# The value product moved behind both score and maximum pairs of a slot, gates of half the tokens, and a projection in four pieces

## The chip, the cores and the metric

One NeuronCore of one Trainium2 chip runs the whole program. The metric is the device time of one launch in microseconds, lower is better. TensorE (PE), VectorE (DVE), ScalarE (ACT) and GpSimd (POOL) each run their own instructions strictly as written, and wait for each other on semaphores; SyncE (SP) issues the transfers.

## The reference

Four sequences of 512 tokens with 128 features pass two layers. In each layer the normalized input goes to an attention and to a feed-forward part, and both are added to the input:

```python
xn = _layernorm(x)
x = x + attn_0(xn) + ffn_0(xn)      # 16 heads of 8, bias; gated feed-forward, hidden 384
xn = _layernorm(x)
x = x + attn_1(xn) + moe(xn)        # 16 heads of 8, block mask; 8 experts of 256, top 2
```

Attention is `softmax(q k^T / sqrt(8)) v` and a projection. The first feed-forward part is `(silu(x Wg) * (x Wu)) Wd`. The second sends each token to the two experts of eight that its router prefers. All is in float32.

## The kernel before

**Units and slots.** The work is cut into eight units (`U = 2 * B`): unit `u` is the attention of sequence `u % 4` in layer `u // 4`. Each unit has 16 slots (`SLOTS_U`), and a slot handles two groups of two heads for one block of 128 keys. In a slot TensorE makes two score pairs (`score_mms`, line 747, two matmuls each, S0 and S1 below), ScalarE takes the exponential of each pair (`exponential`, line 962), and TensorE multiplies the exponentials of the slot before with the values (`value_mms`, line 763, called V below). The exponential needs the maximum of each row beforehand, so in the same slots TensorE makes the scores of a later part a first time (`max_mms`, line 732, M0 and M1 below) and VectorE reduces each pair (`read_max`, line 1114). Maxima run ahead: 24 pairs before the first slot, then two in each slot up to slot 3 of unit 7.

**Three pairs of PSUM banks in turn.** Scores, maxima, gates and expert products all write to banks 0 to 5, in pairs that are handed out in the order of a list, `taken`. Before a job takes a pair, TensorE waits until the job three places earlier in the list has been read:

```python
taken.append(("score", 2 * (SLOTS_U * u + slot) + jj))
if len(pairs_at(u, slot)) > jj:
    taken.append(("max", pairs_at(u, slot)[jj]))
```

So the list reads S0 M0 S1 M1 and then a gate or two expert jobs, if the slot has any. V writes to a bank of its own (6), and all small work (transposes, q, k and v, the projection, routing) goes through bank 7, `SIDE`, at the end of a slot.

**The order on TensorE** is written out by hand in `tensor_unit`: S0, M0, V of the slot before, S1, M1, the gate, expert jobs, and last `side_mms`. In slot 6 two tiles of the projection of the unit before (`out_mms`, lines 822 and 825) stand between V and S1, and the two other tiles at the end of the slot.

**Gates.** In layer 0 each unit has three gate jobs (`gate_up_0`, lines 785 and 786, `HB = 3` blocks of the hidden layer, 512 tokens wide) in slots 9, 10 and 11. ScalarE makes half a tanh (`half_tanh`, line 978), VectorE the rest (`gated`, lines 1135 and 1150), in the slot's last place on both engines.

**ScalarE and VectorE** follow the slots: on ScalarE the first exponential, a copy from bank 7 if there is one, the second exponential, later copies and the tanh; on VectorE the maximum of M0, small work, the maximum of M1, the gate. In slot 6 ScalarE's copy is that of the row maxima (`maxima_copy`, line 955), and the first tile of the projection waits for it, since it overwrites bank 7.

**SyncE's queue** issues all loads of weights before unit 0's own transfers; the last three of `loads` are the experts' weights (`eg`, `eu`, `ed`, 1 MB each), and `max_rows` of unit 0 comes behind them.

**Experts.** From slot 4 of unit 6 each slot has two expert jobs (`expert_work_at`), to slot 11 of unit 7: transposes of gathered tokens (`places_mms`), gates of 320 places (`gate_up_1`, lines 802 and 803) and the output product (`expert_out`, line 810), which ScalarE copies in five pieces (`result_copy`, line 994). In unit 7 from slot 4 there are no maxima.

Of the kernel before, what the change touches and what calls it, by code (L numbers as in the profile page):

```python
# [12 lines left out]
P = 128  # L13
# [4 lines left out]
def build(nc, x, wq, wk, wv, bq, bk, bv, wo, bo, wg_T, wu_T, wd_T, src_blocks, tgt_blocks, router_T, eg_T, eu_T,  # L18
# [4 lines left out]
    U = 2 * B  # L23
# [28 lines left out]
    with ExitStack() as ctx:  # L52
# [114 lines left out]
        emptied = sem("emptied")  # L167
        empty_ready = sem("empty_ready")
        loaded = sem("loaded")
        x_loaded = [sem(f"x_loaded{b}") for b in range(B)]  # L170
        zeros = sem("zeros")
        consts = sem("consts")
# [106 lines left out]
        def pairs_at(u, slot):  # L279

            q = LEAD + PAIRS_U * u + 2 * slot
            return [v for v in (q, q + 1) if v < N_PAIRS]

        def gate_at(u, slot):

            return HB * u + slot - 9 if u < B and 9 <= slot < 9 + HB else None


        expert_work = [("places", 0), ("places", 1)] + [("gate1", m) for m in range(4)]
# [157 lines left out]
        def sync_unit(sp, u):  # L447
            p, n = u + 2, u + 1
            if u == U - 2:
                for e in range(2):  # L450
                    load_places(sp, e)
                load_meta(sp)
                for e in range(2, 4):
                    load_places(sp, e)
            max_rows(sp, u, 1)
            if p < U:
                operand_writes(sp, p, 0)
                operand_writes(sp, p, 1)
                if layer(p) == 0:
                    operand_reads_0(sp, p)  # L460
                else:
                    operand_reads_1(sp, p, 0)
            if u == U - 2:
                for e in range(4, 7):
                    load_places(sp, e)
            if n < U:
                max_rows(sp, n, 0)
            if u == U - 2:
                load_places(sp, 7)
            if p < U and layer(p) == 1:  # L470
                operand_reads_1(sp, p, 1)
            if u < 2:
                empty_places(sp, u)
# [304 lines left out]
            last.then_inc(onT_ps, 1)  # L778

        def gate_up_0(pe, g):  # L780
            u, i = g // HB, g % HB
            pe.wait_ge(ready, 1)
            pair = take_pair(pe, "gate0", g)
            cols = slice(i * P, (i + 1) * P)
            pe.matmul(ps[:, 2 * pair, :], wg[:, cols], xnT[u % 4][:], start=True, stop=True).then_inc(gate_ps[0], 1)  # L785
            pe.matmul(ps[:, 2 * pair + 1, :], wu[:, cols], xnT[u % 4][:], start=True, stop=True).then_inc(up_ps[0], 1)  # L786

        def places_mms(pe, e):
            pe.wait_ge(places_in[e % 2], 16 * (e // 2 + 1))
# [5 lines left out]
        def gate_up_1(pe, g):  # L795

            e, i, c = g // 4, g % 4 // 2, g % 2
            pe.wait_ge(loaded, N_LOAD)
            pe.wait_ge(places_ready, e + 1)
            pair = take_pair(pe, "gate1", g)  # L800
            cols, x_T = slice(i * P, (i + 1) * P), places_T[e % 2][:, c * HALF:(c + 1) * HALF]
            pe.matmul(ps[:, 2 * pair, 0:HALF], eg[:, e, cols], x_T, start=True, stop=True).then_inc(gate_ps[1], 1)  # L802
            pe.matmul(ps[:, 2 * pair + 1, 0:HALF], eu[:, e, cols], x_T, start=True, stop=True).then_inc(up_ps[1], 1)  # L803
# [10 lines left out]
        def out_mms(pe, u, tiles):  # L814
            L = layer(u)
            if tiles[0] == 0:
                pe.wait_ge(onT_ready, u + 1)
                if L == 0:
                    pe.wait_ge(h_ready[0], HB * (u + 1))
            for t in tiles:  # L820
                tok = slice(t * P, (t + 1) * P)
                last = pe.matmul(ps[:, SIDE, tok], o_T[:, tok], w_proj[L][:], start=True, stop=(L == 1))  # L822
                if L == 0:
                    for i in range(HB):
                        last = pe.matmul(ps[:, SIDE, tok], h0_T[:, i, tok], wd[:, i, :], start=False,  # L825
                                         stop=(i == HB - 1))
            if tiles[-1] == NT - 1:
                last.then_inc(y_ps, 1)
# [14 lines left out]
        def side_mms(pe, u, slot):  # L843
# [23 lines left out]
                    pe.wait_ge(qk_f_ready, 2 * p + 2)  # L867
                max_transposes(pe, u, 1)
            if slot == 6 and u >= 1:
                out_mms(pe, w, (2, 3))  # L870
            if slot == 7 and p < U and layer(p) == 1:
                pe.wait_ge(unit_done, u)
                rank_mms(pe, p)
            if slot == 8 and n < U:
                pe.wait_ge(mT_ready, 2 * u + 2)
                pe.wait_ge(unit_done, u)
                if p < U and layer(p) == 1:
                    pe.wait_ge(rank_read, seq(p) + 1)
                v_mms(pe, n, SIDE)
            if slot == 10:  # L880
                pe.wait_ge(unit_done, u)
                if n < U:
                    pe.wait_ge(v_read, n + 1)
                out_transposes(pe, u, 0)
            if slot == 11 and f < U:
                pe.wait_ge(on_ready, 2 * u + 1)
# [12 lines left out]
        def tensor_unit(pe, u):  # L899
# [3 lines left out]
            for slot in range(SLOTS_U):  # L903
# [3 lines left out]
                score_mms(pe, u, slot, 0)  # L907
                if maxima:
                    max_mms(pe, maxima[0])
                if u > 0 or slot > 0:  # L910
                    value_mms(pe, SLOTS_U * u + slot - 1)
                if slot == 6 and u >= 1:
                    pe.wait_ge(mT_ready, 2 * u + 2)
                    out_mms(pe, u - 1, (0, 1))
                score_mms(pe, u, slot, 1)
                if maxima:
                    max_mms(pe, maxima[1])
                if gate_at(u, slot) is not None:
                    gate_up_0(pe, gate_at(u, slot))
                for kind, n in expert_work_at(u, slot):  # L920
# [48 lines left out]

        def half_tanh(act, L, g):  # L970

            n = S if L == 0 else HALF
            act.wait_ge(gate_ps[L], g + 1)
            if g >= 2:
                act.wait_ge(h_ready[L], g - 1)
            elif L == 1:
                act.wait_ge(h_ready[0], HB * B)
            act.activation(th[:, g % 2, 0:n], ps[:, 2 * pair_of(f"gate{L}", g), 0:n], ACT.Tanh, scale=0.5).then_inc(  # L978
                tanh_done[L], 1)

# [38 lines left out]
        def scalar_unit(act, u):  # L1019
            w, n, p, f = u - 1, u + 1, u + 2, u + 3  # L1020
            for slot in range(SLOTS_U):
# [13 lines left out]
                    xnT_copy(act, f, SIDE)  # L1035
                if slot == 14 and n < U:
                    maxima_copy(act, n, 0)
                if slot == 8 and p < U and layer(p) == 1:
# [90 lines left out]
            last.then_inc(on_ready, 1)  # L1129

        def gated(dve, L, g):
            n, bank = S if L == 0 else HALF, 2 * pair_of(f"gate{L}", g)
# [4 lines left out]
            dve.wait_ge(gate_done[L], g + 1)  # L1137
            dve.wait_ge(up_ps[L], g + 1)
            if L == 0:
                if g % HB == 0 and g > 0:  # L1140
                    dve.wait_ge(y_ps, g // HB)
                dst = h0_T[:, g % HB, :]
            else:
                e = g // 4
                if g == 0:
# [38 lines left out]
        def vector_unit(dve, u):  # L1184
            w, n, f = u - 1, u + 1, u + 3
            for slot in range(SLOTS_U):
# [2 lines left out]
                    read_max(dve, maxima[0])  # L1189
                if slot == 2 and u >= 1:  # L1190
                    normalize_out(dve, w, 1)
                if slot == 7 and u >= 1:
                    residual(dve, w)
                if slot == 8 and f < U:
                    statistics(dve, f)
                if slot == 9 and n < U:
                    read_v(dve, n, SIDE)
# [3 lines left out]
                    read_logits(dve, f)  # L1201
                if maxima:
                    read_max(dve, maxima[1])
                if gate_at(u, slot) is not None:
                    gated(dve, 0, gate_at(u, slot))
                for kind, m in expert_work_at(u, slot):
# [3 lines left out]
        def last_vector(dve):  # L1210
            normalize_out(dve, U - 1, 1)
            for b in range(B):
# [16 lines left out]
                 (w_router[:], router_T), (eg[:], eg_T), (eu[:], eu_T),  # L1229
                 (ed[:], ed_T.rearrange("e (b p) d -> p e b d", p=P))]  # L1230
        N_LOAD, N_FIRST = 16 * len(loads), 16 * len(first_loads)
# [279 lines left out]
```

## Time and profile before

| what | value |
|---|---|
| median of three runs | 543.98 us (542.29 to 545.46) |
| the profiled execution's own time | 544.03 us |
| its span, first to last instruction | 542.0 us |
| TensorE busy | 454.8 us (84%) |
| VectorE busy | 400.5 us (74%) |
| ScalarE busy | 328.8 us (61%) |
| GpSimd busy | 262.5 us (48%) |
| granted TensorE clock, mean | 0.95 |

The first score pair starts at 50.0 us, slot 4 of unit 7 at 472.3 us. Busy time counts a matmul to its modelled end, while the next one can start before that. A slot is found in the timeline by its order S0, M0, V, S1, M1.

### The profile page before, as it was taken

Reading aid. Unit: us, or ns where it says so; the run is one execution under the profiler, and the core shown is the slowest. Engines: PE = TensorE matmul, PEld = TensorE weight load, DVE = VectorE, ACT = ScalarE, POOL = GpSimd, SP = SyncE. Lnnn points to the kernel's source line nnn. Section 1 sums busy time; section 2 is a strip of 40 time slices with the busy share of each in tenths; the row PEclk is TensorE's granted clock in tenths of the full one; section 3 lists DMA queues with packets and bytes.
Section 4 is the critical chain, followed back from the end, with each engine's and each line's share of the span. In section 5 each row is a group of like instructions: output and inputs, shape, how many; then the busy total and the mean of one; then the engine's idle time right before and its main releaser. Section 6 shows DMA issues by size and latency. Waiting matters only on the chain.

```text
span 542.0 us, 9302 instructions
## 1 busy us (share of the span) xinstructions
PE 454.8 (84%) x3394; PEld 169.4 (31%) x3394; DVE 400.5 (74%) x538; ACT 328.8 (61%) x422; POOL 262.5 (48%) x499
## 2 busy tenths in 40 slices
PE   3456979889988999899989898987899999999952
PEld 1101213224322433242312431221245453455511
DVE  5699778886998699869887798789876777623204
ACT  2102666776677667656676577777766567667560
POOL 6861263724425562886378657884201233163240
PEclk9755889999999999999999999999999999999995
DMA  3896596244511360626252645174731111010018
GB/s 82 238 230 89 89 343 106 93 163 146 90 43 61 118 62 4 66 72 127 25 52 39 157 43 56 41 160 68 109 52 32 45 50 50 4 44 25 21 47 219
DMA packets 143742, 48.27 MB, mean 89 GB/s; under 512 B 109890, under 2 KB 139090, under 8 KB 142866
## 3 DMA queue, kind: packets, MB, share of 16 engines
q1 hardware_dynamic: 141394, 42.93, 38.1%
q0 software_dynamic: 2304, 4.76, 2.6%
q8 instruction: 27, 0.44, 0.3%
q14 instruction: 17, 0.14, 0.1%
HBM read 22.81 MB, written 23.14 MB: 85 GB/s over the span
## 4 chain that ended last, share of the span: by engine, by line
PE 53%; DVE 18%; issue 10%; ACT 10%; DMA 4%; SPq 4%; POOL 1%; POOLq 0%; ACTq 0%; DVEq 0%
PE ps L763 14%; DVE mx L1114 11%; PE ps L747 9%; PE ps L732 7%; ACT PT L962 6%; PE ps L802 3%; PE ps L810 3%; PE ps L785 2%; PE ps L803 2%; SPq L433 2%; PE ps L693 2%; PE ps L825 2%; PE ps L822 2%; PE ps L786 1%; DVE th L1135 1%
## 5 line engine op out<-in xcount | busy, mean ns | idle before, releaser
L1114 DVE TENSOR_REDUCE mx<-ps 128x2 f32<-128x1024 f32 x256 | 309.4, 1223 | 73.1 <-PE ps L732 65.1
L962 ACT ACTIVATE PT<-ps 128x1024 f32<-128x1024 f32 x256 | 258.6, 1026 | 125.9 <-PE ps L747 116.5
L763 PE MATMUL ps<-PT,Vp 128*32 128x512 f32 x1024 | 138.1, 611 | 5.4 <-ACT PT L962 4.4
L732 PE MATMUL ps<-KO,QO 48*128 48x512 bf16 (+1 forms) x512 | 104.5, 406 | 39.7 <-ACT PT L962 22.6
L747 PE MATMUL ps<-QO,KO 59*128 59x512 bf16 x512 | 100.2, 390 | 3.8 <-DMA QO<-mT 2.5
L520 POOL DMA_INDIRECT y_tokens<-expert_io,meta x40 | 38.6, 964 | 71.5 <-ACT expert_io L994 48.5
L747 PEld LDWEIGHTS ps<-QO,KO 59*128 59x128 bf16 x512 | 24.6, 93 | 142.8 <-issue 87.9
L1135 DVE SCALAR_TENSOR_TENSOR th<-th,ps 128x320 f32<-128x320 f32 (+1 forms) x44 | 23.8, 541 | 35.2 <-ACT th L978 29.4
L732 PEld LDWEIGHTS ps<-KO,QO 48*128 48x128 bf16 (+1 forms) x512 | 25.6, 96 | 70.9 <-ACT PT L962 38.6
L545 POOL CAST mp<-mx 128x32 bf16<-128x32 f32 x16 | 3.4, 214 | 82.9 <-DVE mx L1114 78.7
L509 POOL DMA_INDIRECT x_places<-xe,place_i x32 | 31.9, 995 | 22.3 <-ACT PT L962 15.2
L763 PEld LDWEIGHTS ps<-PT,Vp 128*32 128x32 f32 x1024 | 20.4, 108 | 45.7 <-issue 39.7
L978 ACT ACTIVATE th<-ps 128x320 f32<-128x320 f32 (+1 forms) x44 | 21.1, 487 | 12.0 <-PE ps L802 5.8
L802 PE MATMUL ps<-expert_io,eg 128*128 128x320 f32 x64 | 24.4, 462 | 2.1 <-ACT expert_io L994 0.6
L1150 DVE SCALAR_TENSOR_TENSOR h_all<-th,ps 128x320 f32<-128x320 f32 (+1 forms) x44 | 23.8, 541 | 1.5
L955 ACT COPY mT<-ps 24x512 bf16<-24x512 bf16 x16 | 9.0, 562 | 26.1 <-PE ps L739 26.1
L492 POOL TENSOR_SCALAR xe<-xs,mv,rstd 128x128 f32<-128x128 f32 x28 | 22.2, 802 | 0.8
L994 ACT ACTIVATE expert_io<-ps,meta 128x128 f32<-128x128 f32 x40 | 11.2, 372 | 18.6 <-PE ps L810 18.6
L803 PE MATMUL ps<-expert_io,eu 128*128 128x320 f32 x64 | 22.4, 432 | 0.0
L810 PE MATMUL ps<-ed,h_all 128*128 128x128 f32 x160 | 19.4, 276 | 1.2 <-DVE h_all L1150 1.2
L810 PEld LDWEIGHTS ps<-ed,h_all 128*128 128x128 f32 x160 | 18.9, 192 | 3.0 <-DVE h_all L1150 1.7
L1120 DVE RECIPROCAL rden<-ps 128x32 f32<-128x32 f32 x16 | 5.6, 349 | 16.3 <-PE ps L771 16.3
(166 smaller groups left out, 475.1 us busy)
## 6 DMA issues: line engine op xcount, KB each, us to landing
z<-part SPq DMA_DIRECT2D x16, 384.0 KB
z<-part SPq DMA_DIRECT2D x16, 256.0 KB
QO<-z SPq DMA_DIRECT2D x64, 48.0 KB
KO<-z SPq DMA_DIRECT2D x64, 48.0 KB
x_places<-expert_io SPq DMA_DIRECT2D x2, 1300.0 KB, 7.4
expert_io<-x_places SPq DMA_DIRECT2D x8, 320.0 KB, 3.5
QO<-z SPq DMA_DIRECT2D x6, 384.0 KB
KO<-z SPq DMA_DIRECT2D x6, 384.0 KB
```

The lines of the kernel that those rows point to most:

```text
L509: pool.indirect_dma_start(out=x_places[:], out_offset=bass.IndirectOffsetOnAxis(ap=place_i[:, b, t, k:k + 1], axis=0), in_=xe[p % 2][:, t, ...
L520: pool.indirect_dma_start(out=y_tokens[:], out_offset=bass.IndirectOffsetOnAxis(ap=meta[:].bitcast(I32)[:, e, j, 0:1], axis=0), in_=y_sb[e ...
L732: mm = pe.matmul(ps[:, 2 * pair + half, :], rows_of(QO[u % 3], half, 2 * s + jj, rows, (qt, qt + 1)), rows_of(KO[u % 3], half, 2 * s + jj, ...
L747: mm = pe.matmul(ps[:, 2 * pair + half, :], rows_of(KO[u % 3], half, 2 * s + jj, ROWS, (k, k + 1)), rows_of(QO[u % 3], half, 2 * s + jj, R ...
L763: last = pe.matmul(ps[32 * g:32 * g + 32, PV_BANK, :], Vp[u % 2][:, k, head(s, g), :], PT[:, (2 * t + g % 2) % 4, g // 2, :], start=(s % 2 ...
L802: pe.matmul(ps[:, 2 * pair, 0:HALF], eg[:, e, cols], x_T, start=True, stop=True).then_inc(gate_ps[1], 1)
L803: pe.matmul(ps[:, 2 * pair + 1, 0:HALF], eu[:, e, cols], x_T, start=True, stop=True).then_inc(up_ps[1], 1)
L810: last = pe.matmul(across(pair, j * P, (j + 1) * P), h1_T[:, e % 2, i, j * P:(j + 1) * P], ed[:, e, i, :], start=(i == 0), stop=(i == EB - 1))
L962: act.activation(PT[:, e % 4], ps[:, 2 * pair:2 * pair + 2, :], ACT.Exp).then_inc(exp_done, 1)
L1114: dve.tensor_reduce(mx[:, a, qt, col:col + 5:4], ps[:, 2 * pair:2 * pair + 2, :], AX_X, ALU.max, negate=True).then_inc(max_read, 1)
L1135: dve.scalar_tensor_tensor(out=t, in0=t, scalar=1.0, in1=ps[:, bank, 0:n], op0=ALU.add, op1=ALU.mult).then_inc(gate_done[L], 1)
L1150: dve.scalar_tensor_tensor(out=dst, in0=t, scalar=0.5, in1=ps[:, bank + 1, 0:n], op0=ALU.mult, op1=ALU.mult).then_inc(h_ready[L], 1)
```

## The change

On TensorE, V moves from between M0 and S1 to behind M1, in all slots. The list `taken` keeps its order for scores and maxima.

Each gate job of layer 0 becomes two, for 256 tokens each, and the six stand in slots 10 to 15 in place of three in slots 9 to 11.

For the projection of a layer 0 unit (`spread(u)`, units 1 to 4) the four tiles go to four places: tile 0 in slot 6 between M0 and S1, tile 1 at the end of slot 6, tiles 2 and 3 at the same places of slot 7. With it the residual sum moves from slot 7 to 8, the statistics behind the second maximum of slot 8, and the routing's rank matmuls from slot 7 to 9 (their copy from slot 8 to 10), with the waits that bank 7 then needs. For a layer 1 unit two tiles stand between M0 and S1 of slot 6 and two at its end, as before.

The experts' weights get a semaphore of their own and are loaded in units 0 (`eg`, `eu`) and 1 (`ed`), behind `operand_writes`.

```diff
+        G0, N_TOK0, GATE_SLOT = 2 * HB, S // 2, SLOTS_U - 2 * HB
+        def spread(u):
+            return u >= 1 and layer(u - 1) == 0
+        def rank_slot(u):
+            return 9 if spread(u) else 7
         def gate_at(u, slot):
-            return HB * u + slot - 9 if u < B and 9 <= slot < 9 + HB else None
+            return G0 * u + slot - GATE_SLOT if u < B and slot >= GATE_SLOT else None
...
                 operand_writes(sp, p, 1)
+                if u < 2:
+                    for dst, src in expert_loads[0:2] if u == 0 else expert_loads[2:3]:
+                        sp.dma_start(dst, src).then_inc(experts_loaded, 16)
...
         def gate_up_0(pe, g):
-            u, i = g // HB, g % HB
+            u, i, c = g // G0, g % G0 // 2, g % 2
...
-            pe.matmul(ps[:, 2 * pair, :], wg[:, cols], xnT[u % 4][:], start=True, stop=True).then_inc(gate_ps[0], 1)
+            cols, x_T = slice(i * P, (i + 1) * P), xnT[u % 4][:, c * N_TOK0:(c + 1) * N_TOK0]
+            pe.matmul(ps[:, 2 * pair, 0:N_TOK0], wg[:, cols], x_T, start=True, stop=True).then_inc(gate_ps[0], 1)
...
             if slot == 6 and u >= 1:
-                out_mms(pe, w, (2, 3))
-            if slot == 7 and p < U and layer(p) == 1:
+                out_mms(pe, w, (1,) if spread(u) else (2, 3))
+            if slot == 7 and spread(u):
+                out_mms(pe, w, (3,))
+            if slot == rank_slot(u) and p < U and layer(p) == 1:
                 pe.wait_ge(unit_done, u)
+                if slot > 8:
+                    pe.wait_ge(v_read, n + 1)
                 rank_mms(pe, p)
...
                 if maxima:
                     max_mms(pe, maxima[0])
-                if u > 0 or slot > 0:
-                    value_mms(pe, SLOTS_U * u + slot - 1)
                 if slot == 6 and u >= 1:
                     pe.wait_ge(mT_ready, 2 * u + 2)
-                    out_mms(pe, u - 1, (0, 1))
+                    out_mms(pe, u - 1, (0,) if spread(u) else (0, 1))
+                if slot == 7 and spread(u):
+                    out_mms(pe, u - 1, (2,))
                 score_mms(pe, u, slot, 1)
                 if maxima:
                     max_mms(pe, maxima[1])
+                if u > 0 or slot > 0:
+                    value_mms(pe, SLOTS_U * u + slot - 1)
                 if gate_at(u, slot) is not None:
...
-                if slot == 7 and u >= 1:
+                if slot == (8 if spread(u) else 7) and u >= 1:
                     residual(dve, w)
-                if slot == 8 and f < U:
+                if slot == 8 and f < U and not spread(u):
                     statistics(dve, f)
...
                 if maxima:
                     read_max(dve, maxima[1])
+                if slot == 8 and f < U and spread(u):
+                    statistics(dve, f)
```

## Rows read from the trace of the kernel before

**Rows 1.** The page, part 1: busy time of each engine and share of the span.
```profile
PE 454.8 (84%) x3394; PEld 169.4 (31%) x3394; DVE 400.5 (74%) x538; ACT 328.8 (61%) x422; POOL 262.5 (48%) x499
```

**Rows 2.** Windows: stretch, its length, each engine's busy us, TensorE's clock, DMA share, GB/s.
```profile
49.96:105.90 55.94, 48.68 (x292) 12.59 (x292) 46.11 (x52) 36.27 (x42) 25.01 (x56) 0.90 0.57 139
105.90:161.70 55.80, 51.22 (x346) 17.49 (x344) 46.50 (x57) 38.06 (x45) 19.75 (x41) 1.00 0.42 119
105.90:378.00 272.10, 245.17 (x2032) 81.76 (x2030) 224.57 (x281) 186.71 (x217) 161.07 (x328) 1.00 0.42 83
378.00:472.30 94.30, 88.28 (x685) 41.31 (x683) 72.22 (x100) 62.85 (x95) 20.69 (x31) 1.00 0.27 51
472.30:513.50 41.20, 38.24 (x243) 22.11 (x241) 12.54 (x28) 26.32 (x46) 17.33 (x18) 1.00 0.09 30
513.50:525.50 12.00, 7.64 (x58) 1.40 (x56) 0.00 (x0) 9.04 (x13) 6.73 (x7) 1.00 0.11 38
```

**Rows 3.** Waits of TensorE's matmuls, 50 to 472.3 us: total us, times, longest.
```profile
PE ps L732 <- ACT PT L962: 22.6, 40, 0.8
...
PE ps L747 <- DMA QO<-mT: 2.5, 1, 2.5
...
PE ps L732 <- DMA QO<-mask_q: 0.2, 1, 0.2
```

**Rows 4.** Timeline, unit 1's end: start, duration, engine, instructions merged, idle before.
```profile
161.20 0.39 PE L747 MATMUL ps<-QO,KO 59*128 59x512 bf16 x2
161.43 0.38 PE L732 MATMUL ps<-KO,QO 48*128 48x512 bf16 x2
161.63 1.94 ACT L962 ACTIVATE PT<-ps 128x1024 f32<-128x1024 f32 x2 [0.77 <-PE ps L747]
161.74 0.39 PE L747 MATMUL ps<-QO,KO 59*128 59x512 bf16 x2
161.85 2.52 DVE L1114 TENSOR_REDUCE mx<-ps 128x2 f32<-128x1024 f32 x2 [0.31 <-PE ps L732]
...
162.71 0.39 PE L732 MATMUL ps<-KO,QO 48*128 48x512 bf16 x2 [0.58 <-ACT PT L962]
163.03 1.06 PE L763 MATMUL ps<-PT,Vp 128*32 128x512 f32 x8
...
164.03 0.39 PE L747 MATMUL ps<-QO,KO 59*128 59x512 bf16 x2
```

**Rows 5.** Timeline, the slot behind an expert output product, 431 to 435 us.
```profile
431.58 0.39 PE L747 MATMUL ps<-QO,KO 59*128 59x512 bf16 x2
431.69 1.40 ACT L994 ACTIVATE expert_io<-ps,meta 128x128 f32<-128x128 f32 x5 [2.33 <-PE ps L810]
...
432.95 1.96 ACT L962 ACTIVATE PT<-ps 128x1024 f32<-128x1024 f32 x2
...
434.06 0.39 PE L732 MATMUL ps<-KO,QO 56*128 56x512 bf16 x2 [0.52 <-ACT PT L962]
434.38 0.81 PE L802 MATMUL ps<-expert_io,eg 128*128 128x320 f32 x2
```

**Rows 6.** Timeline, slot 6 of unit 6, 399 to 402 us.
```profile
399.01 0.39 PE L747 MATMUL ps<-QO,KO 59*128 59x512 bf16 x2
...
400.37 0.56 ACT L955 COPY mT<-ps 24x512 bf16<-24x512 bf16 x1
...
400.98 0.71 PE L822 MATMUL ps<-w_proj,o_T 128*128 128x128 f32 x4 [0.36 <-ACT mT L955]
```

**Rows 7.** Windows on the clock: the stretch behind the DMA wait, and the end of unit 1.
```profile
78.00:84.00 6.00, 6.00 (x38) 1.85 (x36) 4.87 (x12) 3.37 (x4) 3.24 (x5) 0.73 0.97 251
157.80:165.50 7.70, 5.79 (x46) 1.16 (x38) 6.64 (x6) 5.92 (x9) 4.91 (x9) 1.00 0.47 179
```

**Rows 8.** Lines with shapes kept apart: gate matmul and VectorE's first gate step.
```profile
L785 PE MATMUL ps<-xnT,wg 128*128 128x512 f32 x24 | 13.2, 632 | 2.2 <-DVE mx L1114 2.2
...
L1135 DVE SCALAR_TENSOR_TENSOR th<-th,ps 128x512 f32<-128x512 f32 x12 | 8.3, 688 | 3.6 <-ACT th L978 3.3
```

More of the change, by code:

```diff
@@ L169, in build @@
         loaded = sem("loaded")
+        experts_loaded = sem("experts_loaded")
         x_loaded = [sem(f"x_loaded{b}") for b in range(B)]
@@ L780, in gate_up_0 @@
         def gate_up_0(pe, g):
-            u, i = g // HB, g % HB
+            u, i, c = g // G0, g % G0 // 2, g % 2
             pe.wait_ge(ready, 1)
             pair = take_pair(pe, "gate0", g)
-            cols = slice(i * P, (i + 1) * P)
-            pe.matmul(ps[:, 2 * pair, :], wg[:, cols], xnT[u % 4][:], start=True, stop=True).then_inc(gate_ps[0], 1)
-            pe.matmul(ps[:, 2 * pair + 1, :], wu[:, cols], xnT[u % 4][:], start=True, stop=True).then_inc(up_ps[0], 1)
+            cols, x_T = slice(i * P, (i + 1) * P), xnT[u % 4][:, c * N_TOK0:(c + 1) * N_TOK0]
+            pe.matmul(ps[:, 2 * pair, 0:N_TOK0], wg[:, cols], x_T, start=True, stop=True).then_inc(gate_ps[0], 1)
+            pe.matmul(ps[:, 2 * pair + 1, 0:N_TOK0], wu[:, cols], x_T, start=True, stop=True).then_inc(up_ps[0], 1)
         def places_mms(pe, e):
@@ L797, in gate_up_1 @@
             e, i, c = g // 4, g % 4 // 2, g % 2
-            pe.wait_ge(loaded, N_LOAD)
+            pe.wait_ge(experts_loaded, N_EXPERT)
             pe.wait_ge(places_ready, e + 1)
@@ L818, in out_mms @@
                 if L == 0:
-                    pe.wait_ge(h_ready[0], HB * (u + 1))
+                    pe.wait_ge(h_ready[0], G0 * (u + 1))
             for t in tiles:
@@ L876, in side_mms @@
                 pe.wait_ge(unit_done, u)
-                if p < U and layer(p) == 1:
+                if p < U and layer(p) == 1 and rank_slot(u) < slot:
                     pe.wait_ge(rank_read, seq(p) + 1)
@@ L883, in side_mms @@
                     pe.wait_ge(v_read, n + 1)
+                if p < U and layer(p) == 1:
+                    pe.wait_ge(rank_read, seq(p) + 1)
                 out_transposes(pe, u, 0)
@@ L970, in half_tanh @@
         def half_tanh(act, L, g):
-            n = S if L == 0 else HALF
+            n = N_TOK0 if L == 0 else HALF
             act.wait_ge(gate_ps[L], g + 1)
@@ L976, in half_tanh @@
             elif L == 1:
-                act.wait_ge(h_ready[0], HB * B)
+                act.wait_ge(h_ready[0], G0 * B)
             act.activation(th[:, g % 2, 0:n], ps[:, 2 * pair_of(f"gate{L}", g), 0:n], ACT.Tanh, scale=0.5).then_inc(
@@ L1037, in scalar_unit @@
                     maxima_copy(act, n, 0)
-                if slot == 8 and p < U and layer(p) == 1:
+                if slot == rank_slot(u) + 1 and p < U and layer(p) == 1:
                     ranks_copy(act, p)
@@ L1131, in gated @@
         def gated(dve, L, g):
-            n, bank = S if L == 0 else HALF, 2 * pair_of(f"gate{L}", g)
+            n, bank = N_TOK0 if L == 0 else HALF, 2 * pair_of(f"gate{L}", g)
             t = th[:, g % 2, 0:n]
@@ L1139, in gated @@
             if L == 0:
-                if g % HB == 0 and g > 0:
-                    dve.wait_ge(y_ps, g // HB)
-                dst = h0_T[:, g % HB, :]
+                if g % G0 == 0 and g > 0:
+                    dve.wait_ge(y_ps, g // G0)
+                dst = h0_T[:, g % G0 // 2, g % 2 * N_TOK0:(g % 2 + 1) * N_TOK0]
             else:
@@ L1228, in build @@
                  (w_proj[1][:], wo[1]), (b_proj[1][:], bo[1][None, :].to_broadcast([P, D])),
-                 (w_router[:], router_T), (eg[:], eg_T), (eu[:], eu_T),
-                 (ed[:], ed_T.rearrange("e (b p) d -> p e b d", p=P))]
-        N_LOAD, N_FIRST = 16 * len(loads), 16 * len(first_loads)
+                 (w_router[:], router_T)]
+        expert_loads = [(eg[:], eg_T), (eu[:], eu_T), (ed[:], ed_T.rearrange("e (b p) d -> p e b d", p=P))]
+        N_LOAD, N_EXPERT, N_FIRST = 16 * len(loads), 16 * len(expert_loads), 16 * len(first_loads)
         def load_x(sp, b):
```

## The prediction

> **What bounds the kernel now.** I read the page first: TensorE is busy 84% of the span, VectorE 74%, ScalarE 61% [rows 1]. No engine is full, so the order of the waits decides. The windows by stretch come next: in unit 1 TensorE is busy 51.22 of 55.80 us and VectorE 46.50 [rows 2], so both are near the end of what they have, and 4.58 us are TensorE's idle time. The waits of TensorE say what that idle time is. Between 50 and 472.3 us the view has 18 rows with 84 waits and 39.9 us in sum, first among them M0's wait for an exponential (40 times, 22.6 us) [rows 3].
>
> The timeline shows the loop behind that wait [rows 4]. S1 is issued at 161.20, ScalarE starts on it at 161.63, TensorE issues M1 at 161.43 and the next S0 at 161.74, then waits until 162.71 for M0, because M0 takes the pair that S1 held. The reader should take four lengths from these rows. A score pair needs 0.23 us until the next pair can be issued (161.20 to 161.43). From a score pair's issue to the issue of the pair that waits for its exponential it is 1.51 us (161.20 to 162.71). From a pair that waited to V it is 0.32 us, and V lasts 1.00 us until the next issue (163.03 to 164.03). The loop S1, exponential, M0, V, S1 is 1.51 + 0.32 + 1.00 = 2.83 us, and TensorE is idle in it unless side work fills the time.
>
> **The change part by part: V behind M1.** By the list `taken`, M0 takes the pair of the S1 before it, and M1 takes the pair of S0 of its own slot (three places back in S0 M0 S1 M1). So M1 can't be issued sooner than 1.51 us behind S0. Before, S0, M0, V and S1 stand ahead of it: 0.23 + 0.32 + 1.00 + 0.23 = 1.78 us, and that wait costs nothing. V is its cover. The trace shows the wait bare in one kind of slot, behind an expert output product: the exponential of S0 starts only after five copies, and M1 is idle 0.52 us for it although V stood ahead of it [rows 5].
>
> After, only S0, M0 and S1 stand ahead of M1, 0.69 us, so TensorE idles some 0.8 us in every slot that has maxima. V is queued behind M1 and can't fill this, nor can the gate, the expert jobs or the side work; and S0 of the next slot is behind all of them. The new loop is S0, exponential, M1, V, gate and side work, next S0: 2.83 us plus all the rest that the slot issues. The old loop is gone, since M0 now comes later than S1's exponential, but it only bound where side work was short; the new one has side work in series.
>
> Without idle time a slot's own five jobs take 0.23 + 0.32 + 1.00 + 0.23 + 0.23 = 2.01 us now, and 2.83 us after: 0.82 us more. There are 116 slots with maxima (units 0 to 6, four of unit 7); the first has no V, which leaves 115 x 0.82 = 94.3 us. From this goes TensorE's present idle time in the same slots: (55.94 - 48.68) + (272.10 - 245.17) + (94.30 - 88.28) = 40.2 us [rows 2]. The idle times are counted from the modelled end of a matmul, 0.39 us, while the next could be issued after 0.23 [rows 4], so each of the 84 waits hides 0.16 us more: 13.4 us. Net: 94.3 - 40.2 - 13.4 = **+40.7 us**. For unit 1 alone, with its ten waits (1.6 us), this gives 51.22 - 1.6 + 16 x 0.82 = 62.7 against 55.80 us.
>
> I take 0.32 us from the pair that waited to V, as the row has it. The Trainium skill (TensorE: Matmul & The Clock Gate, Part 2, step by step) says that TensorE's queue pulls weight loads ahead of matmuls in flight while matmuls keep their order; if V's first weights came early in that way the step would be 0.23, and 115 x 0.09 = 10 us less would give 580. The row speaks against it here.
>
> **Small terms.** (a) In the slot behind an expert output product among those with maxima (four: products in slots 8, 11, 14 of unit 6 and 1 of unit 7) S0 to the first expert job takes 2.80 us now [rows 5]; with V behind M1 it is 3.80, not 2.83: 4 x 0.97 = +3.9. (b) Slot 6: the first projection tiles wait for the row maxima's copy, 1.97 us from S0 [rows 6]; V covered that. In units 5 and 6 the two tiles take 0.71 us, and M1 is issued at 1.97 + 0.71 + 0.23 = 2.91 where the sum has 1.51 + 0.71: +0.7 each, +1.4. In units 1 to 4 a tile has four products, where two products take 0.71 us in the row, so at most 1.4 us; I take 1. Slot 6 loses 0.7 there too, and tile 2 in slot 7 fills the new gap and gives 0.7 back: 0. The split helps only by that. (c) The output copy of slot 0 now starts behind the later V, 0.32 + 1.00 us after M1. A ScalarE copy takes 0.56 us [rows 6], so it ends at 1.88 and with the step to ScalarE at about 1.97, when S0's exponential could start at 1.32 + 0.39 = 1.71: 0.26 us late, seven times: +1.8. (d) In units 1 to 4 the residual and the statistics stand together in VectorE's slot 8 and reach slot 10's maximum late: estimated at 0.4 each, +1.5, with bounds of nothing and one maximum's read, 1.26 [rows 4]. (e) The end, slots 12 to 15 of unit 7, has no maxima; there V ahead of S1 stands in the loop to S1's exponential, and four slots take 12.00 us with 9.04 of ScalarE [rows 2]. After, ScalarE alone bounds, and at most 3.0 us are to be had; the last V has to wait in both orders, so I take less than half, -1.3. (f) The experts' loads no longer stand ahead of `max_rows` of unit 0: the 2.5 us wait goes [rows 3] (it is in the 40.2 already), and with it the time at the lower clock behind it, 0.73 granted in 78 to 84 us [rows 7], (1 - 0.73) x 6.0 = 1.6: -1.6. What waits behind the loads in their new place are unit 2's operand reads and unit 1's row maxima; unit 2's maxima begin at slot 4 of unit 1, past 105.9 us, and the loads are issued in the middle of unit 0. Without that distance the cost would be of the size of the 2.5 us wait.
>
> **Gates in halves.** The matmul columns stay. A half can't take less than half nor more than the whole of 632 ns and 688 ns [rows 8]; I take the lower end plus a little, 0.42 us for each of VectorE's two steps: 12 x 0.42 - 6 x 0.69 = +0.9 us of VectorE per unit, hidden: VectorE has 46.5 busy us in a unit that will last over 60. On TensorE 0 to +3 us over four units; I take 0. The rank matmuls wait for the values' read in slot 9, three units, under 0.3 each: inside (d). Slots 4 to 11 of unit 7 issue the same work in another order and nearly fill TensorE (38.24 of 41.20 [rows 2]): 0, bounds -2 and +2.
>
> Sum: 40.7 + 3.9 + 1.4 + 1.8 + 1.5 - 1.3 - 1.6 = +46.4. The profiled execution took 544.03 us (542.0 of span and 2 around it), which is the median of the runs (543.98). 544.0 + 46.4 = 590.4, and I say **590 us**.
>
> **The rivals.** *Faster: the pair of S0 is free when M1's turn comes.* It decides where 1.51 us or more lie between S0 and M1 without a wait. Then the slot costs 2.01 us and its side work, M0's 22.6 us of waits go [rows 3], VectorE's 0.31 us before each pair too [rows 4], and with the 2.5 and 1.6 of the loads and the 1.3 of the end the time is 544.0 - 28.0 = 516. For it: VectorE idles at present, and S1 and M1 come earlier. Against it: ScalarE's 0.97 us an exponential [rows 4] lies in S0's own slot, and only slots 6 and 7 put anything there. I give it 5 in 100; with 3 more for gains and losses that cancel.
>
> *Smaller: the expert slots escape.* If their gates and copies already pace them so that M1's gap replaces other waits, 20 slots x 0.82 and (a) drop out: 590 - 20 = 570. Against it: TensorE is idle only 6.02 of 94.30 us there [rows 2]. 12 in 100.
>
> *Larger: the clock falls.* TensorE's new gaps of 0.8 us would have it granted 1.2 GHz in part of the time. It had 48.68 + 245.17 + 88.28 = 382 busy us in the slots with maxima [rows 2]; were a tenth of that work at the lower clock, it would take 38 us more: 628. Against it: between 157.8 and 165.5 us TensorE is busy 5.79 of 7.70 us, with a gap in each slot, at clock 1.00 [rows 7]. 8 in 100. The Trainium skill (the same page, A second HAM failure mode: psum-queue depth-cycling) tells of a kernel that cycles through PSUM banks and whose small gaps between groups of matmuls made the clock swing; by that rule this change, with more gaps, is a case for it. The trace so far disagrees, at 1.00 in gaps of that size.
>
> *The move of the loads does nothing*, if another transfer holds the maxima's rows: +4 us, inside the range.
>
> **How the numbers follow.** The forecast has 72 in 100, with its own range of 576 to 606: lower if the step from M1 to V is 0.23 us, as between two other pairs (10 us), and by the bounds of small terms, higher by gates (+3), waits that add up in slots with long side work, and an uneven VectorE. The other cases are 12 (570), 8 (628), 5 (516) and 3 (no change). To leave no more than 2 in 10 outside, the range reaches down to the smaller case: 568 to 606. A measurement of this kernel can tell about 0.5% from no change, 2.7 us. Faster 5, same 3, slower 92 in 100.
>
> **What would show it.** In the profile after: M1 idle before it for ScalarE in nearly every slot with maxima, some 0.6 us in the view's count, over 100 times; M0 waiting for ScalarE no more; slots 0, 3, 5 of a unit over 2.83 us; unit 1 near 62 us; TensorE's busy time nearly unchanged and its share near 77%; slot 6's first tile idle about 1.4 us for the row maxima's copy; no wait for row maxima's transfer in unit 0. The prediction is wrong if M1 is issued right behind S1, or if the clock of the middle stretches is below 1.00.

## Result and the profile after

The change makes the kernel slower: 585.46 us (584.7 to 586.17, four runs) against 544.16 us in the same comparison, a ratio of 1.076 with a 95% interval of 1.073 to 1.080. The forecast was 590, with a range of 568 to 606. The profiled execution has a span of 583.6 us, 41.6 more than before.

The page of the changed kernel, parts 1 and 4: busy time, and the chain that ended last by engine.

```profile
PE 460.2 (79%) x3442; PEld 183.2 (31%) x3442; DVE 403.6 (69%) x562; ACT 327.3 (56%) x434; POOL 261.5 (45%) x499
...
PE 59%; ACT 20%; DVE 9%; issue 7%; DMA 2%; POOL 1%; SPq 1%; POOLq 0%; ACTq 0%; DVEq 0%
```

TensorE's busy time is up by 5 us only [rows 1]; its share fell from 84% to 79%, so what was added is waiting. On the chain ScalarE has 20%, before 10%. Windows of the changed kernel by the same stretches as in [rows 2] (length, busy us of TensorE, weight loads, VectorE, ScalarE, GpSimd, clock, DMA):

```profile
49.96:108.53 58.57, 48.95 (x306) 15.17 (x306) 46.99 (x58) 37.37 (x45) 28.06 (x67) 0.94 0.54 134
108.53:171.17 62.64, 52.53 (x358) 20.17 (x356) 47.34 (x64) 38.08 (x47) 19.51 (x34) 1.00 0.42 124
108.53:408.10 299.57, 246.85 (x2066) 90.77 (x2064) 227.77 (x301) 185.63 (x225) 157.60 (x316) 1.00 0.39 75
408.10:512.00 103.90, 89.01 (x685) 42.13 (x683) 71.19 (x100) 61.66 (x94) 20.59 (x31) 1.00 0.24 46
512.00:555.40 43.40, 39.28 (x243) 22.44 (x241) 12.38 (x27) 26.42 (x47) 17.02 (x18) 0.96 0.08 29
```

| stretch | before | after | difference | the forecast's terms |
|---|---|---|---|---|
| unit 0 | 55.94 | 58.57 | +2.6 | +1.7 |
| units 1 to 5 | 272.10 | 299.57 | +27.5 | +33.1 |
| unit 6 and unit 7 to slot 3 | 94.30 | 103.90 | +9.6 | +12.9 |
| unit 7, slots 4 to 11 | 41.20 | 43.40 | +2.2 | 0 |
| the rest | 78.5 | 78.2 | -0.3 | -1.3 |

(The last column deals the terms of the sum out to their stretches, +46.4 in all. The bounds in the rows lie 0.17 us behind the first score pairs of their stretches; the lengths are right.) The loss is in every stretch that has maxima, and 2.2 us of it in slots of unit 7 that have none. The waits of TensorE's matmuls in the changed kernel, 50 to 512 us, answer to [rows 3]:

```profile
PE ps L746 <- ACT PT L984: 51.8, 83, 0.9
PE ps L836 <- ACT mT L977: 8.1, 6, 1.4
PE ps L761 <- DVE h_all L1172: 7.0, 16, 0.5
```

The first row looks like the old one, 51.8 us in place of 22.6, but it is another wait. In the timeline (slot 1 of unit 2, against [rows 4]) it is seen which:

```profile
173.82 0.39 PE L761 MATMUL ps<-QO,KO 59*128 59x512 bf16 x2
173.96 0.59 ACT L990 COPY o_sb<-ps 128x512 f32<-128x512 f32 x1 [0.49 <-PE ps L777]
174.05 0.38 PE L746 MATMUL ps<-KO,QO 48*128 48x512 bf16 x2
174.28 0.39 PE L761 MATMUL ps<-QO,KO 59*128 59x512 bf16 x2
174.44 1.95 ACT L984 ACTIVATE PT<-ps 128x1024 f32<-128x1024 f32 x2
...
175.52 0.39 PE L746 MATMUL ps<-KO,QO 48*128 48x512 bf16 x2 [0.85 <-ACT PT L984]
175.84 1.07 PE L777 MATMUL ps<-PT,Vp 128*32 128x512 f32 x8
...
176.84 0.66 PE L785 MATMUL ps<-ident,o_sb 128*128 128x128 f32 x4
177.43 0.39 PE L761 MATMUL ps<-QO,KO 59*128 59x512 bf16 x2
```

S0, M0 and S1 are issued 0.23 us apart, then TensorE idles until S0's exponential has ended, issues M1 at 175.52, V, the side work (0.59 us) and only then the next S0. M0 waits no more. Here the gap is 0.85 us, since the output copy, behind the later V, held up S0's exponential; in slots without it the gap reads 0.68. The slots with no side work are 2.83 us long: slot 0 of units 1 to 6, slots 14 and 15 of units 4 and 5, and a few more. Most others have that plus their side work; slot 6 and the expert slots have other waits too.

### The profile page after: what moved, and what is told of

Same layout as the page of the kernel before. It is cut to its first block, busy times and chain, and to the rows that moved or that the text cites. A ratio compares the mean times of both kernels' runs of the same rounds, so it can differ in the third digit from the quotient of the medians.

```text
span 583.6 us, 9474 instructions
## 1 busy us (share of the span) xinstructions
PE 460.2 (79%) x3442; PEld 183.2 (31%) x3442; DVE 403.6 (69%) x562; ACT 327.3 (56%) x434; POOL 261.5 (45%) x499
## 4 chain that ended last, share of the span: by engine, by line
PE 59%; ACT 20%; DVE 9%; issue 7%; DMA 2%; POOL 1%; SPq 1%; POOLq 0%; ACTq 0%; DVEq 0%
PE ps L777 20%; ACT PT L984 17%; PE ps L746 7%; PE ps L761 7%; DVE mx L1136 5%; PE ps L824 3%; PE ps L816 3%; PE ps L799 3%; PE ps L707 2%; PE ps L817 2%; PE ps L839 2%; PE ps L836 2%; PE ps L800 2%; DMA h_all<-y_tokens 1%; PE ps L785 1%
## 5 line engine op out<-in xcount | busy, mean ns | idle before, releaser
L984 ACT ACTIVATE PT<-ps 128x1024 f32<-128x1024 f32 x256 | 255.8, 1027 | 125.6 <-PE ps L761 117.3
L746 PE MATMUL ps<-KO,QO 48*128 48x512 bf16 (+1 forms) x512 | 104.5, 406 | 69.0 <-ACT PT L984 51.8
L761 PE MATMUL ps<-QO,KO 59*128 59x512 bf16 x512 | 98.6, 387 | 16.0 <-DVE h_all L1172 7.0
L1157 DVE SCALAR_TENSOR_TENSOR th<-th,ps 128x320 f32<-128x320 f32 (+1 forms) x56 | 25.7, 459 | 58.7 <-ACT th L1000 50.3
L1000 ACT ACTIVATE th<-ps 128x320 f32<-128x320 f32 (+1 forms) x56 | 23.1, 418 | 39.6 <-PE ps L799 23.5
L1172 DVE SCALAR_TENSOR_TENSOR h_all<-th,ps 128x320 f32<-128x320 f32 (+1 forms) x56 | 25.7, 459 | 1.9
L836 PE MATMUL ps<-w_proj,o_T 128*128 128x128 f32 x64 | 13.9, 327 | 10.9 <-ACT mT L977 9.7
```

The costliest lines, as they stand in the source:

```text
L746: mm = pe.matmul(ps[:, 2 * pair + half, :], rows_of(QO[u % 3], half, 2 * s + jj, rows, (qt, qt + 1)), rows_of(KO[u % 3], half, 2 * s + jj, ...
L761: mm = pe.matmul(ps[:, 2 * pair + half, :], rows_of(KO[u % 3], half, 2 * s + jj, ROWS, (k, k + 1)), rows_of(QO[u % 3], half, 2 * s + jj, R ...
L984: act.activation(PT[:, e % 4], ps[:, 2 * pair:2 * pair + 2, :], ACT.Exp).then_inc(exp_done, 1)
L1172: dve.scalar_tensor_tensor(out=dst, in0=t, scalar=0.5, in1=ps[:, bank + 1, 0:n], op0=ALU.mult, op1=ALU.mult).then_inc(h_ready[L], 1)
```

## Experiments

All of them change only the order, the place or the size of pieces, or repeat one; times stand beside runs of the kernel before on the same chip.

| run | median us | ratio to before, 95% |
|---|---|---|
| V behind M1 alone | 585.93 | 1.078 (1.074 to 1.082) |
| all but V | 536.58 | 0.987 (0.984 to 0.991) |
| changed kernel, V between S1 and M1 | 567.5 | 1.044 (1.040 to 1.048) |
| kernel before, V between S1 and M1 | 568.75 | 1.045 (1.040 to 1.050) |
| loads alone | 540.69 | 0.994 (0.992 to 0.996) |
| gates alone | 539.81 | 0.992 (0.990 to 0.995) |
| projection alone | 547.27 | 1.006 (1.004 to 1.008) |
| kernel before, V between S0 and M0 | 592.92 | 1.090 (1.086 to 1.095) |
| changed kernel, S1 three times | 598.26 | 1.100 (1.097 to 1.103) |
| changed kernel, V early in slot 6 | 578.2 | 1.063 (1.059 to 1.066) |
| V by the kind of slot | 536.95 | 0.988 (0.985 to 0.990) |
| loads and gates | 533.51 (before: 538.94 there) | 0.990 (0.988 to 0.992) |

**V behind M1 alone.**

```diff
                 if maxima:
                     max_mms(pe, maxima[0])
-                if u > 0 or slot > 0:
-                    value_mms(pe, SLOTS_U * u + slot - 1)
...
                 if maxima:
                     max_mms(pe, maxima[1])
+                if u > 0 or slot > 0:
+                    value_mms(pe, SLOTS_U * u + slot - 1)
```

> The kernel before with one edit: V is issued behind M1 in every slot. Theory (M1 waits for the exponential of its own slot's S0, and V was what stood in that time): the same loop of 2.83 us plus side work in every slot with maxima, so unit 1 at 61 to 63 us as in the changed kernel, and 585 to 597 us in all, since the loads' wait in unit 0 (2.5 us) and both first projection tiles between M0 and S1 of slot 6 stay. Rival (the gates in halves and the moved routing and loads carry a part of the loss): 544 to 570 us, unit 1 under 59 us.

585.93 us: the whole loss, with the gates, the projection and the loads untouched. Unit 1 lasts 62.50 us, within 0.2 of the changed kernel. A slot without side work in its timeline, TensorE only:

```profile
170.43 0.39 PE L747 MATMUL ps<-QO,KO 59*128 59x512 bf16 x2
170.66 0.38 PE L732 MATMUL ps<-KO,QO 48*128 48x512 bf16 x2
170.88 0.38 PE L747 MATMUL ps<-QO,KO 59*128 59x512 bf16 x2
171.94 0.39 PE L732 MATMUL ps<-KO,QO 48*128 48x512 bf16 x2 [0.68 <-ACT PT L962]
172.26 1.07 PE L763 MATMUL ps<-PT,Vp 128*32 128x512 f32 x8
173.26 0.39 PE L747 MATMUL ps<-QO,KO 59*128 59x512 bf16 x2
```

From S0 to M1 it is 1.51 us, to V 0.32, to the next S0 1.00: the 2.83 us of the forecast, term for term.

**All but V.** The diff is the change's own without the two hunks above.

> The changed kernel with V back between M0 and S1, everything else of the change kept. Theory: the loss is gone, 536 to 546 us: 4 us from the loads' wait and the lower clock behind it, and the halved gates and the split projection worth between 4 us of gain and 2 of loss. M1's wait for ScalarE is gone and M0's is back. Rival (the other parts carry a part of the loss): 555 to 585 us.

536.58 us, faster than the kernel before by 1.3%. The loss comes with V's move alone. And what the other parts gain by themselves is not seen in the changed kernel, which is no faster than V's move alone (585.46 and 585.93). The slots of the two say why. With V behind M1 slot 7 of unit 0 is 3.09 us long with the loads at their old place, against 2.83: there the late transfer costs 0.3 us and no longer 2.5. Slots 9 to 15 of units 0 to 3 are 0.5 to 0.8 us longer with the gates in halves, and slots 6 and 7 of units 1 to 4 are 0.4 to 0.5 us shorter with the projection in four places. (Of both, 0.17 us in each of units 2 to 4 is the rank matmuls' change of slot.)

**V between S1 and M1**, first in the changed kernel, then in the kernel before.

```diff
                 score_mms(pe, u, slot, 1)
+                if u > 0 or slot > 0:
+                    value_mms(pe, SLOTS_U * u + slot - 1)
                 if maxima:
                     max_mms(pe, maxima[1])
-                if u > 0 or slot > 0:
-                    value_mms(pe, SLOTS_U * u + slot - 1)
```

> The changed kernel with V one place earlier, between S1 and M1. Theory: S0, M0, S1 and V put 1.78 us ahead of M1, more than the 1.51 us that it needs, and V, M1, side work and S0 put as much between S1 and the M0 that waits for it, so both waits go. A slot is then TensorE's own 2.01 us and its side work, or VectorE's two reads of 1.26 us: unit 1 at 50 to 54 us, all 512 to 532 us. Rival (what costs is that V comes late in the slot, so ScalarE's buffers and the output bank come free late): about half way between before and after, 555 to 575 us.

> The kernel before with V between S1 and M1 (in slot 6 the two projection tiles stay ahead of S1), gates, projection and loads as before. Theory: as the run before it, without the 4 us of the loads and with three whole gates: 518 to 538 us, under the kernel before's 544. Rival (V late costs): 550 us or more.

567.5 and 568.75 us: my theory of this place was wrong. M1's wait for ScalarE is gone, as it said, but the kernels are 4% slower than before. The timeline of the second has another wait, S1's for VectorE:

```profile
170.32 0.39 PE L747 MATMUL ps<-QO,KO 59*128 59x512 bf16 x2 [0.89 <-DVE mx L1114]
170.64 1.06 PE L763 MATMUL ps<-PT,Vp 128*32 128x512 f32 x8
...
171.64 0.39 PE L732 MATMUL ps<-KO,QO 48*128 48x512 bf16 x2
...
172.07 2.36 DVE L1114 TENSOR_REDUCE mx<-ps 128x2 f32<-128x1024 f32 x2 [0.68 <-PE ps L732]
...
173.35 0.39 PE L747 MATMUL ps<-QO,KO 59*128 59x512 bf16 x2 [0.20 <-DVE mx L1114]
```

S1 takes the pair of the M1 before it, so it waits until VectorE has read that M1; with V between S1 and M1 the loop read, S1, V, M1, read is 173.35 - 170.32 = 3.03 us. VectorE idles 0.68 us in it. The rival that I had set against it, that V comes late for ScalarE's buffers, isn't what the rows show either; only its number came near. In the first of the two runs slot 6 of unit 7 lasted 11.8 us, with TensorE 4.33 us idle for the row maxima's copy before the projection's first tile; ScalarE had stood still before its tanh and the trace doesn't say why. The granted clock is 0.72 from 497 to 509 us. That slot is 6.6 of the 21 us by which this trace is longer than the one of the kernel before, and the second run has the same wait there, 4.57 us.

**V between S0 and M0** tests the theory that this gave.

```diff
                 score_mms(pe, u, slot, 0)
+                if u > 0 or slot > 0:
+                    value_mms(pe, SLOTS_U * u + slot - 1)
                 if maxima:
                     max_mms(pe, maxima[0])
-                if u > 0 or slot > 0:
-                    value_mms(pe, SLOTS_U * u + slot - 1)
```

> The kernel before with V between S0 and M0. The runs with V between S1 and M1 fell against my theory: VectorE's read of M1 must end before the next S1 may take its pair, and V then stands between that S1 and the next M1, a loop of 1.23 + 0.06 + 0.32 + 1.00 + 0.43 = 3.04 us. The refined theory: there are four such loops, one through each of S0, M0, S1, M1, and V lies in one of them at every place. Between S0 and M0 it is the loop of VectorE's read of M0, the same 3.04 us in plain slots, and in all 560 to 575 us. Rival (the 3.04 us are special to the order of reads on VectorE, where M1 comes second): at or under the kernel before, 544 us or less.

Plain slots are 3.03 to 3.04 us long, as expected, from one S0 that waits for VectorE's read of M0 to the next (the one shown, the last of unit 1, has 3.13); the total, 592.92 us, is above my range of 560 to 575:

```profile
169.50 0.39 PE L747 MATMUL ps<-QO,KO 59*128 59x512 bf16 x2 [0.89 <-DVE mx L1114]
169.82 1.06 PE L763 MATMUL ps<-PT,Vp 128*32 128x512 f32 x8
...
170.82 0.39 PE L732 MATMUL ps<-KO,QO 48*128 48x512 bf16 x2
...
171.25 2.36 DVE L1114 TENSOR_REDUCE mx<-ps 128x2 f32<-128x1024 f32 x2 [0.68 <-PE ps L732]
...
172.63 0.39 PE L747 MATMUL ps<-QO,KO 59*128 59x512 bf16 x2 [0.98 <-DVE mx L1114]
```

A part that I had missed is the slots with gates, 5.0 to 5.5 us each where the kernel before has 4.0 to 5.0: by the list, a gate takes the pair of its slot's M0 and waits for the same read. The waits of that kernel have TensorE idle for VectorE before the gate's matmul (line 785) 10.7 us, before 2.2 [rows 8]. The twelve slots are 10.4 us longer in all. That is not the whole: units 5 and 6 have no gates of layer 0, and they are 4.8 and 7.2 us longer than before, with waits for VectorE before side work and expert jobs. How much each of these adds was not separated.

**Loads, gates and projection, each alone** (the diffs are the change's own hunks).

> The kernel before with the move of the experts' loads alone. Theory: unit 0 loses the wait for the row maxima's transfer and the lower clock behind it, 55.98 to about 52.1 us as in the run of all but V; the rest stays: 539 to 542 us. Rival (another transfer holds those rows): 543 to 545 us.

540.69 us, as expected. Unit 0 shrinks from 55.97 to 53.22 us, and its slot 7 from 5.54 to 2.87.

> The kernel before with the gates in halves alone. Theory (the same columns on TensorE, 0.9 us more on VectorE a unit, spread over six slots): slots 8 to 15 of units 0 to 3 at 28 to 29 us as before, 542 to 546 us. Rival (three more evictions and waits a unit cost in series): 4 x 2 us, 550 us or more.

539.81 us, better than I expected. Slots 8 to 15 of unit 1 are as long as before (28.4 and 28.3 us); the gain is in slots 0 and 1 of the next unit, 5.73 us where unit 1 had 6.55, and some 3.0 us over units 1 to 4. By the list a gate in slot 15 turns the order of pairs, so that the next M0 takes the pair of the M1 before and not that of S1. The timeline agrees: in slot 0 of unit 1 M0 is issued at 106.69 us, 0.22 behind S0 and with no wait, where the kernel before has TensorE idle 0.63 us for ScalarE. No run separates the place of the gates from their size.

> The kernel before with the projection in four places and the moved residual, statistics and rank work alone. Theory: VectorE and ScalarE get their next pair sooner in slot 6, and units 1 to 4 gain 0.3 to 1.5 us each: 539 to 543 us. Rival (the later residual delays the values and the routing behind it): 546 us or more.

547.27 us, 0.6% slower: the wrong way. Slots 6 and 7 together take 8.9 to 9.0 us in units 1 to 4; the kernel before has 8.5 in unit 1 and 9.2 in units 2 to 4, so 0.4 us is lost once and 0.2 gained three times. The profiled executions differ by 2.4 us, and 1.9 of that is one slot, slot 8 of unit 4 (6.51 us against 4.58), where TensorE stands still 2.1 us among the matmuls of the values and the profile names nothing that it waits for. Whether the other executions have that stop isn't known; why this part costs 3.8 us in the medians stays open.

**S1 three times in the changed kernel**, the measured size of the gap.

```diff
         def score_mms(pe, u, slot, jj):
...
-            for half in range(2):
+            for half in [0, 1] * (3 if jj == 1 and pairs_at(u, slot) else 1):
```

> The changed kernel with the matmuls of S1 issued three times in slots with maxima (the same values to the same pair), 0.46 us more of TensorE's work between M0 and M1 in 116 slots. Theory (TensorE idles there for S0's exponential): M1's turn comes at 0.23 + 0.23 + 0.69 = 1.15 us, still under 1.51, so plain slots stay at 2.83 us; only slots 6 and 7 with a projection tile ahead of S1 and some expert slots pay: 588 to 598 us. Rival (the changed kernel is bound by TensorE's work, which its order only makes dearer): 116 x 0.46 = 53 us more, 638 us.

598.26 us: 12.8 more, where 116 slots got 0.46 us of work each. TensorE in slot 1 of unit 2:

```profile
177.62 0.39 PE L761 MATMUL ps<-QO,KO 59*128 59x512 bf16 x2
177.85 0.38 PE L746 MATMUL ps<-KO,QO 48*128 48x512 bf16 x2
178.07 0.81 PE L761 MATMUL ps<-QO,KO 59*128 59x512 bf16 x6
179.33 0.39 PE L746 MATMUL ps<-KO,QO 48*128 48x512 bf16 x2 [0.44 <-ACT PT L984]
179.65 1.06 PE L777 MATMUL ps<-PT,Vp 128*32 128x512 f32 x8
```

The six matmuls fit in the gap, which is still 0.44 us, and plain slots stay at 2.83 us. What was paid lies in the slots that the forecast of this run named, slots 6 and 7 (0.43 each) and the expert slots, and in the first two slots of unit 0 (1.7 us), which it had not named. So three quarters of the extra work cost nothing: the changed kernel isn't bound by TensorE's work.

**V early in slot 6 of the changed kernel**, at its old place there alone.

```diff
+                if slot == 6 and (u > 0 or slot > 0):
+                    value_mms(pe, SLOTS_U * u + slot - 1)
                 if slot == 6 and u >= 1:
...
-                if u > 0 or slot > 0:
+                if slot != 6 and (u > 0 or slot > 0):
                     value_mms(pe, SLOTS_U * u + slot - 1)
```

> The changed kernel with V at its old place in slot 6 of every unit alone, where the first projection tile waits for the copy of the row maxima. Theory (V covered that wait): slot 6 gets 1.0 us shorter in units 1 to 6 and 2.6 us in unit 7, where the clock fell too; 8.6 us less, 575 to 579 us. Rival (that wait is hidden by M1's own): under 1.5 us less, 584 us or more.

578.2 us, 7.3 less. Slot 6 goes from 5.68 to 4.68 us in units 1 to 4, from 4.78 to 3.79 and from 6.94 to 5.94 in units 5 and 6, and from 7.78 to 5.15 in unit 7: V covered the wait for the row maxima's copy, 1.0 us each time. The other 1.6 us in unit 7 are the lower clock of the changed kernel there; the run of V alone has the same late V and a clock of 1.00 in that slot, and it takes 6.14 us.

**V by the kind of slot**: all but V, and V behind S1 where a slot has no maxima, except slot 6.

> All parts of the change but with V between M0 and S1 in every slot with maxima and in slot 6, and behind S1 in the slots without maxima (unit 7 from slot 4). Theory: the plain V rule of the run of all but V, 536.6 us, less 0.3 to 1.0 us that the late V gained in slots 4 to 15 of unit 7: 535 to 537 us. Rival (the gain at the end came from elsewhere): no less than 536.5 us.

536.95 us, which the medians don't tell from 536.58, and which fits both the theory's range and the rival's. The traces tell more. From the first score pair of slot 12 of unit 7 to the last V it is 8.87 us, where all but V has 10.91; from the same score pair to the end of the span it is 28.3 and 28.4 us. So the late V does shorten the last slots by 2.0 us, and the end doesn't come sooner.

**Loads and gates**, the two parts that gain alone.

> The kernel before with the loads' move and the gates in halves, V and the projection as before. Theory (the two gains of 2.8 and 3.7 us lie in different slots and add, and the split projection gave nothing: alone it cost 3 us, and in slots 6 to 10 of unit 1 the run of all but V took 19.37 us and that of the gates alone 19.18): 535 to 538 us, the same as the run of all but V, 536.6. Rival (the split projection pays once the gates leave slot 9): 539 us or more.

Its chip ran the kernel before in 538.94 us, so the number to read is the ratio, 0.990 (0.988 to 0.992); its interval overlaps that of all but V, 0.987 (0.984 to 0.991). On the chip of that run it would be some 538 us, at the upper end of the range that I gave. Leaving the projection in two places costs nothing that these runs can tell. These three versions with V at its old place beat both kernels, by 1.0 to 1.3% of the first.

## Why the prediction was right

**The mechanism held step by step.** M1 waits for S0's exponential of its own slot, 1.51 us from issue to issue; V is queued behind it and side work behind V; M0's wait is gone; the run of V alone has the whole loss. From an M1 that waited to V it is 0.32 us in the changed kernel too (175.52 to 175.84), and V's first weight load has its row at 175.84, so the head start that the Trainium skill (TensorE: Matmul & The Clock Gate, Part 2) gives to weight loads is not seen there. Between S0 and M0 it is: M0's weights are loaded at 173.83 and its matmul is issued at 174.05.

**The number is nearer than its terms.** 590 lies within 5 us of the result because misses of both signs partly cancel: the term for all slots and (d) below were too large, the gates, the end and slot 6 of unit 7 cost more than forecast. That part is luck.

**The term for all slots, +40.7 us, was too large, by about 5 us in units 1 to 5.** I took 0.82 us per slot. That holds between two pairs, but where side work follows M1 the step from M1 to it is 0.31 us already before, and 1.00 behind V after (175.84 to 176.84), so such a slot pays 0.74. In units 1 to 5 the trace has side work in 67 of 80 slots, which makes 5.4 us; 33.1 and 27.5 are 5.6 apart, and the other misses there, (c), (d) and the gates, about cancel. That is a count from two rows; no run tests it.

**Small terms.** (a) The slot behind an expert product: S0 to the first expert job was to take 3.80 us. The rows of the changed kernel against [rows 5]:

```profile
466.17 0.39 PE L761 MATMUL ps<-QO,KO 59*128 59x512 bf16 x2
...
467.73 0.39 PE L761 MATMUL ps<-QO,KO 59*128 59x512 bf16 x2 [0.95 <-ACT expert_io L1016]
468.64 0.39 PE L746 MATMUL ps<-KO,QO 56*128 56x512 bf16 x2 [0.52 <-ACT PT L984]
468.96 1.06 PE L777 MATMUL ps<-PT,Vp 128*32 128x512 f32 x8
...
469.96 0.81 PE L816 MATMUL ps<-expert_io,eg 128*128 128x320 f32 x2
```

It is 469.96 - 466.17 = 3.79. The "smaller" rival was right in part all the same: slots 7, 10 and 13 of unit 6 changed by +0.22, -0.16 and +0.22 us only, having waited for VectorE or ScalarE in another place before, and the stretch grew by 9.6 us, not 12.9.

(b) Slot 6, against [rows 6], here in unit 1:

```profile
129.00 0.39 PE L761 MATMUL ps<-QO,KO 59*128 59x512 bf16 x2
...
130.35 0.56 ACT L977 COPY mT<-ps 24x512 bf16<-24x512 bf16 x1
130.97 0.49 PE L836 MATMUL ps<-w_proj,o_T 128*128 128x128 f32 x2 [1.36 <-ACT mT L977]
```

1.97 us from S0 to the first tile, 1.36 idle (forecast 1.4). What I overlooked is unit 7, where the same wait stands without maxima around it: 1.0 us more in slot 6 (5.15 before, 6.14 in the run of V alone). With the 1.6 us of the lower clock there it is more than the +2.2 us that slots 4 to 11 had in place of 0; without the clock's part they have +0.5 in the run of V alone.

(c) The output copy: slot 1 pays 0.19 us, not 0.26.

(d) VectorE's late statistics: slots 8 to 10 of unit 1 have 3.92, 2.83 and 4.32 us, what the loop and side work give alone. Slot 9 is 3.17 us in units 3 and 4 and 2.99 in unit 2, with the rank matmuls in it; so under 0.5 us in all in place of +1.5.

(e) The end gained 0.1 us, not 1.3, and here a step was wrong: I let ScalarE's exponentials bound it. They do come sooner: from the first score pair of slot 12 to the last V it is 8.87 us (555.24 to 564.11) where it was 10.91 (513.55 to 524.46). But the chain that ended last goes another way in both kernels. It leads through seven transfers of expert results (five of the last expert, two of the one before) that GpSimd starts one by one, 1.26 us apart, the last 10.26 us behind that score pair (565.50) where it was 10.29 (523.84).

(f) The loads: the wait is gone; alone they were worth 2.8 us, where the two parts in the forecast made 4.1: the slot behind the wait is 0.7 us shorter in that run (4.70 and 3.97), not 1.6. And with V's move all but 0.3 us of the wait is gone even with the loads at their old place, since slot 7 of unit 0 then comes later.

**Gates in halves** were taken at 0, with 0 to +3 us as bounds. VectorE's two steps came out as assumed, 0.42 us each. But against the run of V alone slots 9 to 15 are 0.5 us longer in units 1 to 3 without the rank matmuls' share, and 0.7 in unit 0: some 2 us in all. That the gates gain by themselves, 3.7 us, was not foreseen.

**The clock rival** came true in one place and not at large: the stretches of units 1 to 6 have 1.00. By that, the trace disagrees with the Trainium skill (TensorE: Matmul & The Clock Gate, A second HAM failure mode: psum-queue depth-cycling), which has the clock swing with small gaps between groups of matmuls. In slot 6 of unit 7 the clock did fall:

```profile
521.71 0.39 PE L761 MATMUL ps<-QO,KO 59*128 59x512 bf16 x2
...
523.67 0.71 PE L836 MATMUL ps<-w_proj,o_T 128*128 128x128 f32 x4 [1.57 <-ACT mT L977]
...
524.63 1.82 PE L777 MATMUL ps<-PT,Vp 128*32 128x512 f32 x8
```

V takes 1.82 us there in place of 1.06, and the window around it reads:

```profile
521.70:529.60 7.90, 6.33 (x33) 3.52 (x33) 1.87 (x6) 3.63 (x5) 2.87 (x3) 0.78 0.11 38
```

The lower clock cost 1.6 us, the difference to the same slot in the run of V alone (7.77 and 6.14). The view's count of waits was off: 83 waits of M1 are put down to the matmul, where I said over 100, and 104 to its weight load. TensorE's share is 79%, where I said 77%.

## What to carry to other kernels

With three buffers handed out in turn to four jobs a slot, each job closes a loop: its own issue, the reader of its buffer, the job three places on. Before moving a long instruction in an in-order queue, write down these loops with their measured steps and ask in which of them it lies at the new place, and what it covered at the old. Here all four places put V in one loop, and the old one costs least, 2.83 us with side work running inside the wait, against 2.83 with side work in series, 3.03 and 3.04. And run the parts of a change alone: the loads and the gates gained 0.6 and 0.8% by themselves, the projection lost 0.6%, and V's move hid all three.

## What the runs showed of the hardware

In unit 7, slot 6, of the changed kernel TensorE's granted clock fell to its lower level (1.2 GHz) after a single wait of 1.57 us, while gaps of 0.7 to 0.85 us in most slots for 300 us left it at 1.00. Where it falls isn't fixed by the order of instructions. The run of V alone has the same wait of 1.57 us in the same slot, and there the clock stays at 1.00 (519 to 527 us) and V takes 1.06 us; the run with S1 three times has that wait too, and the clock fell (0.81 from 534 to 543 us). And in the run with V early in slot 6, the slot behind an expert product (waits of 0.95 and 0.52 us, as in the changed kernel) was followed by slow matmuls, and lasted 7.84 us in place of 6.14:

```profile
459.80:467.70 7.90, 6.42 (x27) 3.02 (x26) 3.42 (x4) 4.03 (x9) 2.93 (x3) 0.78 0.07 25
```

Two exponentials in a row on ScalarE take 1.94 us [rows 4], and one alone, in the next slot of the same timeline, 1.02.
